# The second layer's feed-forward is started inside the last units of the cross attention of the same layer

## What is computed

```python
def _L1_xattn_ref(x, cond, Wq, bq, Wkv, bkv, Wp, bp):   # 16 heads of 16 channels, all 1024 tokens against all 1024 keys
    ...
    q = _fq_sym(q, axis=-1); k = _fq_sym(k, axis=-1); v = _fq_sym(v, axis=2)
    attn = jax.nn.softmax(jnp.einsum('bhqd,bhkd->bhqk', q, k), axis=-1)
    attn = _fq_unsigned(attn, axis=-1)
    out = jnp.einsum('bhqk,bhkd->bhqd', attn, v)
    return out @ Wp + bp

def _L1_ffn_ref(x, lut, gate_idx, up_idx, down_idx):     # 688 hidden channels, weights lut[idx]
    gate = _ghost_linear(x, gate_idx, lut)
    up = _ghost_linear(x, up_idx, lut)
    h = jax.nn.silu(gate) * up
    return _ghost_linear(h, down_idx, lut)

def _L2_attn_ref(x, pre_norm_w, w_a, w_i, w_v, ...):     # the third layer's recurrence
    h = _rmsnorm(x, pre_norm_w)
    a = jax.nn.sigmoid(h @ w_a + decay_bias); i_gate = jax.nn.sigmoid(h @ w_i); v = h @ w_v
    ...
# the third layer's feed-forward has ternary weights; they depend on nothing but the weights:
    gamma_w = jnp.clip(jnp.mean(jnp.abs(w)), 1e-05, None)
    w_dq = jnp.clip(jnp.round(w / gamma_w), -1.0, 1.0) * gamma_w

x = x + _L1_xattn_ref(_layernorm(x), ctx_2048, ...)
x = x + _L1_ffn_ref(_layernorm(x), ...)
x = x + _L2_attn_ref(_layernorm(x), ...)
```

## Time and profile before

| | |
|---|---|
| three runs | 1705.3, 1700.36, 1710.93 us |
| median | 1705.3 us |
| profiled execution | 1706.57 us, its span 1705.2 us |
| granted TensorE clock, mean | 0.864 |
| PE busy | 1439.1 us (84%) |
| DVE busy | 1134.8 us (67%) |
| ACT busy | 795.0 us (47%) |
| POOL busy | 762.6 us (45%) |

### The profile page before, as it was taken

One profiled execution on the slowest core, in us unless ns is written; L12 is line 12 of the kernel. 1 busy time (PEld: TensorE's weight loads), 2 busy tenths in 40 slices (PEclk: granted clock), 3 DMA queues, 4 the chain that ended last, 5 costly groups with the idle time before them and its releaser, 6 DMA issues. The chain is left out here.

```text
span 1705.2 us, 25406 instructions
## 1 busy us (share of the span) xinstructions
PE 1439.1 (84%) x8102; PEld 1034.1 (61%) x8102; DVE 1134.8 (67%) x2958; ACT 795.0 (47%) x2000; POOL 762.6 (45%) x1217
## 2 busy tenths in 40 slices
PE   6999978799999979999897795376877678769999
PEld 4676654688888723333576684155555455548888
DVE  7877776377776588989366447778878478943223
ACT  3444432144343478878315224576656367741110
POOL 4888861175656467667222215255555323320000
PEclk9999997999999965555799897587877789979999
DMA  8000002000000056555500000203232075310000
GB/s 288 1 8 8 1 14 105 14 1 8 7 1 1 1 102 103 87 91 93 201 1 1 1 0 4 105 1 62 41 47 50 1 165 117 54 13 1 7 7 13
DMA packets 168835, 77.84 MB, mean 46 GB/s; under 512 B 156928, under 2 KB 161408, under 8 KB 167552
## 3 DMA queue, kind: packets, MB, share of 16 engines
q1 hardware_dynamic: 168704, 76.23, 19.6%
HBM read 37.40 MB, written 1.05 MB: 23 GB/s over the span
## 5 line engine op out<-in xcount | busy, mean ns | idle before, releaser
L101 PE MATMUL banks<-normed_t,arena_a 128*128 128x256 f32 x1120 | 257.7, 386 | 5.3 <-PEq L3534 5.3
L101 PEld LDWEIGHTS banks<-normed_t,arena_a 128*128 128x128 f32 x1120 | 216.6, 194 | 36.4 <-issue 6.5
L465 POOL TENSOR_TENSOR lut_weights<-lut_weights,arena_b 128x536 f32<-128x536 f32 x128 | 181.2, 1416 | 122.5 <-DVE arena_b L455 113.3
L598 POOL TENSOR_SCALAR work<-work,small 128x256 f32<-128x256 f32 (+1 forms) x384 | 176.2, 476 | 70.6 <-DVE small L590 70.4
L101 PE MATMUL banks<-arena_a 64*128 64x512 bf16 (+1 forms) x384 | 161.5, 539 | 14.9 <-ACT arena_a L1743 8.4
L1743 ACT ACTIVATE arena_a<-banks,work 128x1024 uint8<-128x1024 f32 x128 | 154.0, 1204 | 40.3 <-DVE work L1683 33.9
L1681 DVE TENSOR_REDUCE work<-banks 128x1 f32<-128x1024 f32 x128 | 155.4, 1214 | 19.6 <-PE banks L101 19.4
L107 PE MATMUL banks<-identity,work 128*128 128x128 f32 x968 | 138.5, 285 | 25.9 <-ACT work L543 10.8
L1779 POOL TENSOR_SCALAR arena_a<-arena_a 128x1024 bf16<-128x1024 uint8 x128 | 132.3, 1045 | 54.9 <-DMA arena_a<-arena_a 53.3
L578 ACT ACTIVATE work<-banks,small 128x256 f32<-128x256 f32 (+1 forms) x258 | 114.9, 452 | 83.5 <-DVE small L565 55.7
L107 PEld LDWEIGHTS banks<-identity,work 128*128 128x128 f32 x968 | 116.0, 148 | 49.4 <-POOL work L598 26.9
(11 more groups left out here) (463 smaller groups left out, 3197.5 us busy)
## 6 DMA issues: line engine op xcount, KB each, us to landing
arena_a<-in_L3f_wg SPq DMA_DIRECT2D x8, 512.0 KB, 4.0
arena_b<-in_lut_idx SPq DMA_DIRECT2D x8, 268.0 KB, 2.8
arena_b<-in_L_wqn SPq DMA_DIRECT2D x4, 512.0 KB, 9.7
arena_b<-in_L_wo SPq DMA_DIRECT2D x4, 512.0 KB, 13.1
arena_a<-in_L_wq SPq DMA_DIRECT2D x1, 2048.0 KB, 7.5
arena_a<-in_L_wo SPq DMA_DIRECT2D x1, 2048.0 KB, 12.7
arena_a<-arena_a SPq DMA_TRANSPOSE x128, 2.5
arena_b<-in_L2f_gv SPq DMA_DIRECT2D x1, 2048.0 KB, 8.2
```

Source lines behind the costliest of these rows:

```text
L101: ins = t.matmul(out, lhs_t, rhs, start=start and i == 0, stop=stop and i == n - 1)
L465: g.tensor_tensor(o, o, lut_t[j % 2], ALU.add).then_inc(*summed.up(c * LUT + j))
L598: ins = g.tensor_scalar(e[:, c], e[:, c], A.rl[n % 2][:, 2 * hh + i:2 * hh + i + 1], 0.0, ALU.mult, ALU.add)
```

## The change

The stage `l1_ffn` loses its place in `STAGES` and the barrier ahead of it. `l1_cross` asks for its generators and runs them item by item: TensorE's items 0 to 3 (gates, ups, and for item 3 the down product of batch 0) stand behind the mixes of loop steps 129, 132, 135 and 138; VectorE's and ScalarE's parts follow one step later; the rest comes after the loop. The first three items wait for the last exponentials that used their PSUM pairs. Batch 3's norm is moved into item 4. GpSimd runs `rec_gpsimd(n)` ahead of `ternary_gpsimd(n)`. The ternary steps on VectorE now stand at q = 5: A0, 6: B0, 7: C0, 8: D0 A1, 9: B1 C1, 10: D1 A2, 12: B2 C2, 13: D2. SyncE's loads wait for the residual of the last tile. The barrier at the end of the feed-forward stays.

```diff
@@ l1_cross @@
+        items_tensor, items_vector, items_scalar, ffn_gpsimd, ffn_sync = l1_ffn()
+        ALL_ITEMS = 2 * NB * NJ1
@@ tensor @@
-            yield MEET
+                if n in (129, 132, 135, 138):
+                    yield from some(items_tensor, 1)
+            yield from some(items_tensor, ALL_ITEMS)
@@ vector @@
-            yield MEET
+                if n in (130, 133, 136, 139):
+                    yield from some(items_vector, 1)
+            yield from some(items_vector, ALL_ITEMS)
@@ scalar @@
-            yield MEET
+                if n in (130, 133, 136):
+                    yield from some(items_scalar, 1)
+            yield from some(items_scalar, 1)
+            yield from norm_scalar("l1f", big_a, None, [3], both=True)
+            yield from some(items_scalar, ALL_ITEMS)
@@ gpsimd @@
-            yield MEET
+            yield from ffn_gpsimd()
@@ sync @@
-            yield MEET
+
+            sp.wait_ge(*(yield added, s, NT - 1))
+            yield from ffn_sync()
@@ l1_ffn @@
+        def pair(q):
+
+            return 2 * (q % 3), [(gated_, s, q - 3)] if q >= 3 else [(exped, "l1x", H * NT - 3 + (q - 2) % 3)]
+
         F = Gated(s, NJ1 // 2, NB, gates, ups, pieces, [big_b[:, i * NJ1 * S:(i + 1) * NJ1 * S] for i in range(2)], down, lambda g: g,
-                  lambda b: (xt_a, s, b), lambda g: (xt_a, REC, "rec", g - 2) if g >= 2 else (xt_a, s, g + 2))
+                  lambda b: (xt_a, s, b), lambda g: (xt_a, REC, "rec", g - 2) if g >= 2 else (xt_a, s, 3) if g else (added, "l1x", NT - 2), pair)
@@ tensor @@
-                if q == 0:
+                if q == 4:
                     yield from norm_tensor(s, nf, high, [3], by_scalar=True)
                 if q in (6, 9, 12):
                     yield from rec_turn_tensor("rec", q // 3 - 2)
+                yield None
@@ vector @@
-                if q >= 3:
-                    yield from some(back, 2 if q % 3 == 2 else 1)
+                if q >= 5:
+                    yield from some(back, (1, 1, 1, 2, 2, 2, 0, 2, 2)[q - 5])
+                if q < 4:
+                    yield None
@@ scalar @@
-
-            yield from norm_scalar(s, nf, None, [3], both=True)
-            yield from turned_scalar(s, 3, high)
+                if q == 4:
+                    yield from turned_scalar(s, 3, high)
+                yield None
+
@@ gpsimd @@
             for n in range(3):
+                yield from rec_gpsimd(n)
                 yield from ternary_gpsimd(n)
-                yield from rec_gpsimd(n)
             yield MEET
...
-        return tensor, vector, scalar, gpsimd, sync
+        return tensor(), vector(), scalar(), gpsimd, sync
...
-    STAGES = [l0_attention, l0_cross, l0_ffn, l1_attention, l1_cross, l1_ffn,
+    STAGES = [l0_attention, l0_cross, l0_ffn, l1_attention, l1_cross,
               l2_attention, l2_cross, l2_ffn, l3_attention, l3_cross, l3_ffn]
```

More of the change, by code:

```diff
@@ L1829, in build, with __init__ @@
     class Gated:
-        def __init__(self, s, per, groups, gates, ups, pieces, hid, down, batch, turned, emptied):
+        def __init__(self, s, per, groups, gates, ups, pieces, hid, down, batch, turned, emptied, pair=None):
+            self.pair = pair or (lambda q: (2 * (q % 3), [(gated_, s, q - 3)] if q >= 3 else []))
             self.s, self.per, self.groups, self.n = s, per, groups, per * groups
@@ L1852, in gated_tensor @@
                     t.wait_ge(*(yield F.turned(b)))
-                if q >= 3:
-                    t.wait_ge(*(yield gated_, F.s, q - 3))
+                pair, free = F.pair(q)
+                for done in free:
+                    t.wait_ge(*(yield done))
                 for c, w_ in enumerate(F.gates(q)):
-                    ins = products(t, banks[q % 3 * 2].f[0:w_(0).shape[1], c * S:(c + 1) * S], [(w_(k), of_batch(b, k)) for k in range(KH)])
+                    ins = products(t, banks[pair].f[0:w_(0).shape[1], c * S:(c + 1) * S], [(w_(k), of_batch(b, k)) for k in range(KH)])
                 ins.then_inc(*hid_gate.up(F.s, q))
                 for c, w_ in enumerate(F.ups(q)):
-                    ins = products(t, banks[q % 3 * 2 + 1].f[0:w_(0).shape[1], c * S:(c + 1) * S], [(w_(k), of_batch(b, k)) for k in range(KH)])
+                    ins = products(t, banks[pair + 1].f[0:w_(0).shape[1], c * S:(c + 1) * S], [(w_(k), of_batch(b, k)) for k in range(KH)])
                 ins.then_inc(*hid_up.up(F.s, q))
@@ L1874, in gated_vector @@
             if q < F.n:
-                o, up = F.hidden(q), banks[q % 3 * 2 + 1].f
+                pair = F.pair(q)[0]
+                o, up = F.hidden(q), banks[pair + 1].f
                 v.wait_ge(*(yield silued, F.s, q))
@@ L1878, in gated_vector @@
                 for cols, _, r in F.pieces(q):
-                    ins = v.tensor_tensor(o[r, cols], o[r, cols], (banks[q % 3 * 2].f if r.start else up)[r, cols], ALU.mult)
+                    ins = v.tensor_tensor(o[r, cols], o[r, cols], (banks[pair].f if r.start else up)[r, cols], ALU.mult)
                 ins.then_inc(*gated_.up(F.s, q))
@@ L1894, in gated_scalar @@
                 for cols, src, dst in F.pieces(q):
-                    ins = a.activation(F.hidden(q)[dst, cols], banks[q % 3 * 2].f[src, cols], ACT.Silu)
+                    ins = a.activation(F.hidden(q)[dst, cols], banks[F.pair(q)[0]].f[src, cols], ACT.Silu)
                 ins.then_inc(*silued.up(F.s, q))
```

## The result

The changed kernel takes 1722.9 us (median of 14 runs, 1713.65 to 1730.4), the kernel before 1710.6 (median of 14 on the same chips, 1700.36 to 1715.94). The ratio is 1.0064 with a 95% interval of 1.0045 to 1.0082, so some 10.9 us more, interval 7.7 to 14.0 (the two medians lie 12.3 apart). The forecast of 1720 us was right in sign and mechanism; its +14.6 us lie just beyond the upper end. The profiled execution took 1726.96 us, its span 1725.6, mean granted clock 0.859.

The account below looks back on a forecast made before the run. TensorE is the busiest engine, but GpSimd's chain of norms and all-reduces decides when the last norms come. Batch 3's turn 12.6 us later plus 2.0 for the clock gives +14.6 on 1705.3: 1719.9, say 1720; range 1706 to 1726.

Parts of the forecast that it names:

- The two causes: Feed-forward: loads issued 13.9 us later hold rec_vector(0); one more all-reduce on GpSimd's chain makes batch 3's turn 12.6 us late.
- the lead: Ahead of batch 0's turn: TensorE, full from 819.5 on, would be done at 859.9, 7.0 us sooner than before.
- the wait and its clock: Ahead of batch 0's turn: TensorE idles 7 us for rec_vector(0), and its fallen clock costs 2.0 us more.
- the switches and what follows from them: GpSimd's code switches, 6.0 us into an all-reduce and 7.1 back, the last behind the barrier: batch 3's turn 12.6 us later.
- The front: Cross attention's end: TensorE is full from 819.5 on, item 4 starts near 843.5, item 6's down product ends at 859.9.
- The loads: Behind the last tile's residual: first issue at 844.1, 13.9 us later; the nine tensors land at 866.1, holding rec_vector(0).
- The clock: TensorE's clock falls in the idle times ahead of batch 0's and batch 3's turns: 2.0 us each, bounds 0 and 2.2.
- the second lull: TensorE idles 5 us ahead of batch 3's turn and its clock falls once more: 2.0 us, bounds 0 and 2.2.
- GpSimd's chain: Norm, blank, all-reduce, blank, norm with one more all-reduce: barrier at 911.9, 7.5 us later, batch 3's turn at 922.9.
- the middle one: One cause doesn't bind: way back runs during the barrier wait, +6.1, or nine loads land 7 us sooner, +3 to +6; 0.18.
- the collisions: Slower rival: rec_gpsimd(1), (2) and (3) take 5.0 to 6.0 us each under VectorE's steps, up to 6 us more, 1726; 0.12.
- TensorE's list: Fast rival: TensorE's list alone sets the pace and the lead of 7 us reaches the end, 1698; chance 0.08.

Follow-up runs that it names:

- one switch: All three sums first, then three all-reduces in a row: in the kernel before, ratio 0.9955; in the changed kernel, 0.9978; there with the nine loads first too, 0.9911.
- nine loads first: The changed kernel, but SyncE issues the next stage's nine loads once the last unit is mixed, ahead of the ternary ones: ratio 1.0057.
- the two edits show +6.0 and +6.1: The changed kernel with the next stage's nine loads issued ahead of the ternary ones, 1.0057; the changed kernel with item 3 behind the last tile's output product, 1.0054.
- the two edits show +6.9 and +9.5: The changed kernel with all-reduces 1 and 2 in a row, batch 2's norm after them, 1.0031; with a tiny GpSimd instruction behind all-reduce 2, 1.0026.
- the kernel with both causes removed: The changed kernel with three all-reduces in a row and the next stage's nine loads issued ahead of the ternary ones: ratio 0.9911, 1694.4 us.
- item 3 last: The changed kernel, but item 3 with batch 0's down product stands behind the last tile's output product, not ahead of it: ratio 1.0054.
- the two named above: The changed kernel with the nine loads issued ahead of the ternary ones, 1.0057, and with a tiny GpSimd instruction behind all-reduce 2, 1.0026.

## Why the prediction was right

**The two causes.** Both were named beforehand with their place, and each was taken away alone. From the first marks follows a balance in three terms. The items in TensorE's pauses, with the barrier that goes and all else in the change, are worth 6.8 us (-12.2 against -5.4, both with one switch and without late loads). The late loads cost 9.2 (-3.0 against -12.2). The switches, with the order of VectorE's steps that goes with them, cost 16.7 behind the change (+13.7 against -3.0) and 5.4 before, so the change makes them 11.3 dearer. Sum: -6.8 + 9.2 + 11.3 = +13.7. That the sum comes out is no proof: the terms are differences of the same marks and must close. The split also depends on the order: with all switches in place the early loads gave 7.8, not 9.2. Read in the same three terms, the forecast had -7.0 for the lead, 7.0 + 2.0 for the wait and its clock, and the rest of its +14.6, 12.6, for the switches and what follows from them. The first two terms lie within 0.2 us of the measured ones; the third, a remainder on both sides, is 1.3 too high.

**The front.** Forecast of item 4 843.5, seen 842.7; of TensorE being ready for the turn 859.9, seen 859.3. The gain was real; the changed kernel doesn't keep it.

**The loads.** Forecast: first issue 844.1, last landing 866.1. On the clock of before the issue came at 843.45 and L1964 began at 865.5. The step that mattered was to look for what else waited behind the residual of the last tile, and who read it.

**The clock.** The turn and the 44 records behind it took 12.27 us to the next down product (870.56 to 882.83); in the kernel with nine loads first 9.99 (870.66 to 880.65). The fall cost 2.3 us, forecast 2.0, just above the bound of 2.2. Behind the second lull the shift grew from +12.0 at the turn to +13.7 at the first mark, so 1.7 for a forecast of 2.0. The forecast had only these two lulls. It didn't name the waits of 5.12 and 5.77 us at 900.52 and 915.53; they didn't change the sum, since GpSimd and VectorE set the pace there.

**GpSimd's chain.** On the clock of before: `rec_gpsimd(1)` 876.7 (forecast 876.7), end of all-reduce 1 886.9 (887.1), `rec_gpsimd(2)` 895.7 (896.0), barrier 911.2 (911.9), `rec_gpsimd(3)` 918.4 (918.9), turn of batch 3 922.3 (922.9). The way back behind the barrier took 7.1 us, forecast 7.0. The way back is 6.77 to 7.56 us in six of the experiments (7.16, 6.96 and 6.95 in the rows above), so its 7 was rightly taken from the row. The Trainium skill (GPSIMD Engine Reference, Instruction dispatch) has the first call to a freshly loaded kernel pay some 6 us that show as no instruction; the way in agrees here, with 5.84 and 5.69.

**What was off.** The whole time moved by 10.9 where the stretch moved by 13.6. Since the interval reaches to 14.0, the two don't contradict each other, and no run here tells whether later stages give some of it back. The base was off too: 1705.3 was the median of three runs, 1710.6 that of fourteen, so that 1720 came so near 1722.9 is in part luck, two errors of opposite sign: the base 5.3 too low, the shift 3.7 too high. The rivals did not come true. The two halves of the middle one can be held against the experiments: for loads that land 7 us sooner it gave +3 to +6 us, and the two edits show +6.0 and +6.1 in the stretch; for a way back that doesn't stand behind the barrier it gave +6.1, and the two edits show +6.9 and +9.5. Of the collisions there was one, in the norm that starts at 880.79 (4.0 us, the others 3.0). The way back doesn't run while GpSimd waits at the barrier; it did so only when an ordinary instruction stood ahead of it. And TensorE's list comes near to setting the pace alone only in the kernel with both causes removed.

## What to carry to other kernels

When work is moved forward, list everything that stood behind it in program order, above all DMA issues tied to its end, and look for the first reader of each: a lead on the busiest engine lasts only until the first wait for something that the same edit made later. An engine that alternates between two kinds of work, as GpSimd does between all-reduces and small ordinary instructions, should do all of one kind in a row, as far as what it depends on allows; the blank between kinds shows only as idle time with no releaser, and it must not be the first thing behind a barrier. A change that fails can be half right: here the moved items are worth 6.8 us in the stretch once the two waits are gone.

## What the runs showed of the hardware that was not expected

- The way into the all-reduce, 5.7 to 6.1 us when the DMA engines are idle, took 9.59 us while they were full (DMA share 1.05 in the window from 859.80, which lies in it), and 9.53, 10.11 and 10.51 in the three experiments with the same late loads. With item 3 last the loads end earlier within it (share 0.96 in its first 2.1 us, 0.26 in the next 2, then 0.02), and the way in took 7.54. Behind the change it was hidden.
- All-reduces in a row cost 0.38 to 0.41 us each, with no load between them, even when GpSimd waits 1.79 us or 7.00 us for VectorE in between.
- TensorE's granted clock was still 1.00 through 5.10 us of idle time ahead of the turn of batch 3, and fell only in the matmuls behind it (0.63); ahead of the turn of batch 0 it fell within the 7.20 us (0.62). Even the same short wait ends in two ways: behind 1.96 us of idle time ahead of the last down product the clock was 1.00 in the changed kernel with one switch (6.04 us for the 24 records), and 0.66 in the first 2.6 us with the loads first as well (7.68 us). What decides this was not tried.
- The same lull of 10.4 us in the third layer (ahead of 963.18 behind the change) is followed by low-clock stretches of unequal length: eight records that come 6 us later took 1.89 us in eight of the ten profiled kernels, the one before among them, and 3.62 in the two named above. With the records around them this moves a profiled execution by 3 us.
